# Moving the high and low parts of v into a block diagonal by DMA in place of engine copies, in a fused attention and feed-forward kernel

## The reference

```
xn = layernorm(x)
q, k, v = xn @ wq.T + bq, xn @ wk.T + bk, xn @ wv.T + bv      # (b, s, 32 heads, 32)
scores  = einsum('bshd,bstd->bsht', q, k) / sqrt(32)           # heads against heads, of ONE token
probs   = softmax(scores, axis=-1)
context = einsum('bsht,bstd->bshd', probs, v)
x = x + context
x = x + ffn(layernorm(x))      # base matmul + top-2 of 8 experts' rank-16 LoRA
```

## Time and profile before

| | |
|---|---|
| median of 3 runs | 1345.84 us |
| the profiled execution | 1345.48 us, its span 1343.3 us |
| mean granted clock | 0.985 |
| PE busy | 1238.6 us, 92% of the span |
| DVE busy | 1143.1 us, 85% |
| ACT busy | 669.8 us, 50% |
| POOL busy | 262.7 us, 20% |
| L325 on ACT | 384 copies, 235.9 us, 614 ns each |
| DMA | 33.1% of 16 engines' time, mean 90 GB/s |

### The profile page before, as it was taken

How to read it: one execution, slowest core, us unless ns; L and a number is a source line. 1 busy time by engine, 2 the same in 40 slices (tenths; PEclk the granted TensorE clock), 3 DMA queues, 4 the chain that set the end, 5 groups by cost and what they waited for, 6 DMA issues and landing times.

```text
span 1343.3 us, 29100 instructions
## 1 busy us (share of the span) xinstructions
PE 1238.6 (92%) x11920; PEld 622.0 (46%) x11920; DVE 1143.1 (85%) x1533; ACT 669.8 (50%) x982; POOL 262.7 (20%) x246
## 2 busy tenths in 40 slices
PE   0677899999999999999999999999999999999994
PEld 0253444554444445544444455444444454444442
DVE  5658889888898898888988988889889888898883
ACT  8964455444544554445445544454455444544540
POOL 0020222211112222111122222121222221212220
PEclk9898999999999999999999999999999999999997
DMA  9631333333223333332233333322333333223221
GB/s 350 246 94 42 85 78 78 94 94 92 62 76 82 78 78 94 94 93 62 76 82 78 78 94 94 93 61 75 82 78 78 94 94 94 62 75 82 63 55 40
DMA packets 167667, 120.91 MB, mean 90 GB/s; under 512 B 141408, under 2 KB 142432, under 8 KB 167648
## 3 DMA queue, kind: packets, MB, share of 16 engines
q1 hardware_dynamic: 167648, 120.66, 33.1%
HBM read 53.51 MB, written 16.78 MB: 52 GB/s over the span
## 4 chain that ended last, share of the span: by engine, by line
issue 60%; POOL 14%; ACT 10%; DMA 7%; DVE 4%; PE 3%; POOLq 0%; DVEq 0%; ACTq 0%
DMA x_hi<-row_hi 7%; POOL work L500 5%; POOL work L488 4%; ACT work L616 3%; ACT row_hi L612 3%; ACT row_hi L599 2%; DVE work L772 2%; POOL columns L483 1%; POOL columns L476 1%; PE dense_acc L1093 1%; PE acc L1033 1%; PE acc L1042 1%; ACT row_hi L618 0%; ACT columns L614 0%; ACT w_hi_k L567 0%
## 5 line engine op out<-in xcount | busy, mean ns | idle before, releaser
L1093 PE MATMUL dense_acc<-base_parts,x_hi 128*128 128x512 f16 x1024 | 305.8, 380 | 0.0
L325 ACT COPY work<-work 32x512 f16<-32x512 f16 x384 | 235.9, 614 | 9.9 <-POOL work L494 1.2
L1093 PE MATMUL dense_acc<-base_parts,x_lo 128*128 128x512 f16 x512 | 194.5, 380 | 0.0
L599 ACT CAST row_hi<-work 128x1024 f16<-128x1024 f32 x32 | 33.5, 1046 | 286.7 <-DVE work L772 286.7
L1033 PE MATMUL acc<-w_hi_k,x_hi 128*128 128x512 f16 x512 | 124.5, 387 | 48.0 <-DVE w_lo_k L733 34.7
L806 DVE SCALAR_TENSOR_TENSOR work<-acc,acc_to_a,biases_sb 128x512 f32<-128x512 f32 x192 | 143.5, 748 | 21.8 <-PE acc L1042 15.7
L1093 PEld LDWEIGHTS dense_acc<-base_parts,x_hi 128*128 128x128 f16 x1024 | 99.6, 100 | 110.0 <-issue 1.0
L1033 PE MATMUL acc<-w_hi_q,x_hi 128*128 128x512 f16 x512 | 123.9, 386 | 12.1 <-DVE work L806 9.3
L1033 PE MATMUL acc<-v_parts,x_hi 128*128 128x512 f16 x512 | 121.0, 379 | 0.7 <-DVE work L806 0.7
L1042 PE MATMUL acc<-w_hi_q,x_lo 128*128 128x512 f16 x512 | 121.5, 380 | 0.0
L1042 PE MATMUL acc<-w_hi_k,x_lo 128*128 128x512 f16 x512 | 121.2, 380 | 0.0
(11 more groups left out here) (145 smaller groups left out, 2042.8 us busy)
## 6 DMA issues: line engine op xcount, KB each, us to landing
work<-x_dram SPq DMA_DIRECT2D x64, 512.0 KB, 3.3
work<-work SPq DMA_DIRECT2D x256, 64.0 KB, 2.0
out_dram<-work SPq DMA_DIRECT2D x32, 512.0 KB, 2.7
work<-wT_dram SPq DMA_DIRECT2D x19, 512.0 KB, 10.8
v_parts<-wT_dram SPq DMA_DIRECT2D x8, 512.0 KB, 6.8
base_parts<-wT_dram SPq DMA_DIRECT2D x5, 512.0 KB, 15.9
biases_sb<-bias_dram SPq DMA_DIRECT2D x4, 512.0 KB, 11.5
x_hi<-row_hi SPq DMA_TRANSPOSE x64, 3.1
```

The costliest lines, as they stand in the source:

```text
L325: copy(diag[c * QD:(c + 1) * QD, :, c, j::NQ, :], src).then_inc(vdiag_ready, 1)
L599: nc.scalar.copy(row_hi[:, :], xn).then_inc(row2_hi, 1)
L1093: nc.tensor.matmul(dense_acc[n][:, :], rows_part[:, k, :], w_part[:, k, cols], start=(k == 0 and m == 0), stop=False)
```

## The change

The 16 copies become 16 DMAs on SyncE, behind the transposing DMAs for the next tile and ahead of the store of y. They wait for the same two semaphores as ScalarE's copies did, `v_lo_ready` and `scored`. A DMA counts 16 on its semaphore, so the waits on `vdiag_ready` are for 16 times as much. So that each (c, j) is a contiguous run of 8 x 32 numbers (512 B) on both sides, v's parts are written in another order, [part, c, f, 32] with token t = 4f + c, and the slots of `diag` for v are j * 8 + f in place of j + 4f; `attend` takes its slice of `diag` by a function that differs between scores and context. The number and the sizes of all matmuls are as before. ScalarE's and VectorE's copies are gone, with no other instruction in their place.

```diff
-        v_parts_t = k_parts.rearrange("p a t c -> p (a t c)").rearrange("p (t a c) -> p t a c", t=QD, a=2)
+        v_parts_t = k_parts.rearrange("p a (f q) c -> p a (f q c)", q=NQ).rearrange(
+            "p a (q f c) -> p a q f c", q=NQ, c=QD)
...
-        C_ACT_FIRST, C_ACT_LAST, C_DVE = (0, 1), (2,), (3,)
-
-        def spread_v(copy, c):
-
-            for j in range(NQ):
-                src = v_parts_t[j * QD:(j + 1) * QD, c::NQ, :, :].rearrange("p t a c -> p a t c")
-                copy(diag[c * QD:(c + 1) * QD, :, c, j::NQ, :], src).then_inc(vdiag_ready, 1)
+        turned_v = turned.rearrange("p (f q c) -> p q f c", q=NQ, c=QD)
...
+            def spread_v(t):
+
+                sp.wait_ge(v_lo_ready, t + 1)
+                sp.wait_ge(scored, t + 1)
+                f = QD // NQ
+                for c in range(NQ):
+                    for j in range(NQ):
+                        sp.dma_start(diag[c * QD:(c + 1) * QD, :, c, j * f:(j + 1) * f, :],
+                                     v_parts_t[j * QD:(j + 1) * QD, :, c, :, :]).then_inc(vdiag_ready, 16)
...
                     turn1_lo(t + 1)
+                spread_v(t)
                 if prev:
 
                     sp.wait_ge(base_free, 2 * t + 2)
...
-                nc.gpsimd.tensor_tensor(v_parts_t[:, :, 1, :], turned3, v_parts_t[:, :, 0, :],
+                nc.gpsimd.tensor_tensor(v_parts_t[:, 1, :, :, :], turned_v, v_parts_t[:, 0, :, :, :],
...
-                nc.scalar.copy(v_parts_t[:, :, 0, :], turned3).then_inc(v_hi_ready, 1)
+                nc.scalar.copy(v_parts_t[:, 0, :, :, :], turned_v).then_inc(v_hi_ready, 1)
...
-                act.wait_ge(v_lo_ready, t + 1)
-                act.wait_ge(scored, t + 1)
-                for c in C_ACT_FIRST:
-                    spread_v(nc.scalar.copy, c)
...
-                for c in C_ACT_LAST:
-                    spread_v(nc.scalar.copy, c)
...
-                for c in C_DVE:
-                    spread_v(nc.vector.tensor_copy, c)
...
-                pe.wait_ge(vdiag_ready, 4 * NQ * (p + 1))
+                pe.wait_ge(vdiag_ready, 16 * 4 * NQ * (p + 1))
                 pe.wait_ge(p_lo_ready, p + 1)
-                attend(ctx_acc)
+                attend(ctx_acc, lambda i4, c: c * (QD // NQ) + i4)
```

More of the change, by code:

```diff
@@ L640, in step @@
                 if prev:
-                    act.wait_ge(vdiag_ready, 4 * NQ * t)
+                    act.wait_ge(vdiag_ready, 16 * 4 * NQ * t)
                 nc.scalar.copy(k_parts[:, 0, :, :], turned3).then_inc(a_hi_ready, 1)
@@ L1055, in _, with attend @@
             terms = ((0, 0), (0, 1), (1, 0))
-            def attend(done):
+            def attend(done, spread_at):
                 for i4 in range(QD // NQ):
@@ L1063, in attend @@
                             mm = nc.tensor.matmul(attn_ps[c * QD:(c + 1) * QD, i4 * P:(i4 + 1) * P],
-                                                  dense_parts[:, i, dense_part, :], diag[:, spread_part, :, i, :],
+                                                  dense_parts[:, i, dense_part, :],
+                                                  diag[:, spread_part, :, spread_at(i4, c), :],
                                                   start=(n == 0), stop=(n == len(terms) - 1))
@@ L1164, in step @@
                 pe.wait_ge(b_lo_ready, t + 1)
-                attend(scored)
+                attend(scored, lambda i4, c: i4 * NQ + c)
                 if prev:
```

## The result

The changed kernel takes 1353.08 us (median of 5 runs, 1351.42 to 1353.68), the kernel before 1345.58 us (1344.07 to 1347.09) beside it: a ratio of 1.0053, 95% interval 1.0043 to 1.0064, slower by 7.5 us. The profiled execution has a span of 1350.3 us, 7.0 more than before. One execution of experiment 7 took 3369.5 us and is left out of its median.

What follows compares the result with a forecast made beforehand. TensorE, busy 98.67 of 100 us, was taken to bound the kernel. 1345.48 - 0.2 (first tile) + 6.0 (steady tiles) + 0.6 (last tile) = 1351.9, left at 1351.5 us; range 1343 to 1379.

Steps and rivals of the forecast that it cites:

- The likeliest case: Before the context's matmuls: the sixteen DMAs land 0.1 to 0.6 us late a tile, 1348 to 1365 us; chance 0.43.
- Issue time: On SyncE's queue: 0.64 us a DMA, beside 0.63 for k's spreading; first step 0.57, landing 2.05.
- rival (b): On SyncE: the two-run shape costs more to issue, at 0.70 us +1.05 a tile, 1378 us; chance 0.20.
- Rival (a): Before the context: the DMAs land before TensorE's turn and are hidden, 1344.3 to 1347 us; chance 0.30 (within 0.2%).
- Rival (c): On GpSimd: v's low part, written contiguously, is 0.3 us shorter and shortens TensorE's gap, 1336 us; chance 0.07.
- A steady tile: At the context: the sixteenth DMA is seen at 735.0 against 734.76, +0.2 us a tile, +6 over thirty.
- one wrong zero: At the dense term with `low`: ScalarE's copy of `low` moves up about 2 us and gains TensorE 0.
- 0.08 at most: At the context's first weight load: TensorE's most possible loss to the engine copies in a tile, in us.
- The last tile: At its context, with no projection ahead: TensorE starts at 1308.7 in place of 1308.13, +0.6 us.
- The first tile: VectorE's copies gone bring the base weights' scale and cast forward: -0.2 us once; the DMAs themselves cost 0.
- Nothing on ScalarE and VectorE: 7.6 us of ScalarE's and 1.24 of VectorE's work go a tile, gaining 0 beyond the first tile's -0.2.
- the gap: Before the transpose of `low`: TensorE idles 0.66 us behind VectorE's 128x1 instruction; forecast to stay 0.66.

Runs made afterwards that it cites:

- experiment 7: The changed kernel with GpSimd's bias addition to x1 held back until VectorE has written `low`: 1350.38 us, ratio 1.0049 to the kernel before.
- experiment 1: The kernel before with only the new order of v's parts and `diag` slots, all 16 copies still on ScalarE and VectorE: 1345.04 us, ratio 1.0002.
- experiment 3: The changed kernel with twelve DMAs a tile on SyncE and the other four copies on VectorE: 1341.47 us, ratio 0.9969 to the kernel before.
- experiment 2: The changed kernel with its sixteen DMAs split, eight issued by SyncE and eight by ScalarE: 1341.43 us, ratio 0.9970 to the kernel before.
- experiment 6: The kernel before with GpSimd's bias addition to x1 held back until VectorE has written `low`: 1343.07 us, ratio 0.9980.
- experiment 9: The kernel before with GpSimd's bias addition held back and ScalarE's copy of `low` between its first and second four copies of v: 1317.30 us, ratio 0.9785.
- experiment 8: The changed kernel with twelve DMAs on SyncE, four copies on VectorE, and GpSimd's bias addition held back: 1313.90 us, ratio 0.9763 to the kernel before.

## Why the prediction was right

**The sum.** Forecast 1351.5 us, measured 1353.1; forecast +6, measured +7.5. The likeliest case came true, by its mechanism: the landing of sixteen DMAs, 0.64 us apart, sets the context's start. That the size fits so well is partly luck. The prediction added 6.0 for the steady tiles; without the pauses they cost 4.1, and the pauses, which it did not have, brought 3.1.

**Issue time.** 0.64 taken, 0.64 measured; the first step was 0.70 in place of 0.57 and the landing 1.9 in place of 2.05, and that these two errors cancel is luck. The new shape, two runs and half of k's bytes, takes some 0.006 us more an issue than k's (0.639 and 0.633), so rival (b) is out. Rival (a) failed by only 0.2 us of a train of 11.6. Rival (c) needed GpSimd's low part to be at least 0.1 us shorter; it is 0.007 shorter (experiment 1).

**A steady tile.** +0.20 forecast, +0.14 measured. The train costs 0.2 against TensorE's turn; the 0.06 come back at ScalarE's copy of `low`. That is the prediction's one wrong zero ("L1100 already runs without a gap, so 0"): the first matmul was on time, the second was not (0.48 us behind the first, now 0.43). The "0.08 at most" at the context, on the other hand, was really zero.

**The last tile.** +0.6 forecast, +0.66 measured. **The first tile.** -0.2 forecast, about -0.6 measured for the whole stretch, which differs by 0.3 between the kernel before (53.91) and experiment 1 (53.63), where the same copies are on the engines. The forecast term itself can be seen: from ScalarE's cast of the probabilities to GpSimd's maximum of the base weights (106.66 and 109.33 before, 106.42 and 108.89 after) it is 2.47 us in place of 2.67, and with VectorE's copies kept in experiments 1 and 3 it is 2.67. The other 0.4 lie elsewhere, and no run tells their cause.

**What was missing.** The five pauses in the train, 3 us. The prediction said that SyncE's queue was free and priced the train as undisturbed; it did not ask what pauses SyncE makes on its own that its idling had hidden. One could be seen in the kernel before, too: at 746.77 a step of k's spread is 0.94 us in place of 0.63, and a packet of q14 follows at 748.4.

**Nothing on ScalarE and VectorE.** 7.6 and 1.24 us a tile were forecast to go, 7.3 and 1.15 of busy time went, and for it TensorE's period fell by 0.06 in experiment 2: right in the changed kernel. Experiments 6 and 9 limit it: once the gap is gone, the order on ScalarE is worth 0.9 us a tile (38.37 and 37.45).

**Issuing engines, and the gap.** In these runs the issue time makes the train: fifteen steps of 0.64 us, and 1.9 once for a landing. The Trainium skill (DMA: Bandwidth & Descriptors, Issuing engines are not separate DMA queues) says that issuing from several engines saves only the sequencer's time, which is usually small beside the DMA itself. Experiment 2 agrees that this is what is saved, but in a string of small DMAs it was not small: 0.64 a DMA is a third of its landing, and the split saved 11.6 us in all. For the gap, the multiply on 128x1 took 2.0 us beside GpSimd's addition and 0.16 us without it. The Trainium skill (SBUF — State Buffer, SBUF: two separate sides) describes the pair of ports that VectorE and GpSimd share as an exclusive lock held for a whole instruction. The trace agrees: the multiply and GpSimd's addition end within 0.02 us of each other, and L984 shows the same once more in experiment 8, with 2.03 us in place of 1.22.

## What to carry to other kernels

A string of small DMAs on one queue lasts its number times the issue step (here 0.63 to 0.65 us for 32 partitions, from two runs of 64 B to one of 2 KB on each) and one landing (1.9): lay that against the time until the consumer comes before moving copies there, and if it misses by little, shorten the string or split it between two queues. Work taken from an engine that bounds nothing returns nothing; look first for the gaps of the engine that does, here 0.8 us a tile from a one-column instruction beside a long one of GpSimd. When one wait is removed the next may stand right behind it with the same length, so change both before judging either.

## What was not expected of the hardware

- Issues on ScalarE's queue ran while its own activation was still executing (721.77 against an end at 722.49).
- One step in a string of issues was longer by 0.3 us in four tiles of thirty, and one issue by 1.3 us in a fifth, each next to a packet on an "instruction" queue, and in the same tiles again in experiment 7.
- A DMA of 64-byte runs was issued no faster than one of 2 KB runs (two in 1.30 us, against steps of 0.63).
